# Seven VectorE instructions in place of seven transfers for the column shifts of a deformable convolution's offsets

## What is computed

```python
def deform_conv(x, dw, pw, pwb, w, b):
    f = lax.conv_general_dilated(x, dw, (1, 1), 'SAME', feature_group_count=C, ...)   # 7 x 7, by channel
    off = lax.conv_general_dilated(f, pw, (1, 1), 'SAME', ...)                        # 1 x 1, C -> 18
    off = (off + pwb[None, :, None, None]) * OFFSET_SCALE
    py = yy + ky + off[:, :, 0]          # for each of the 9 taps of each pixel: where to sample
    px = xx + kx + off[:, :, 1]
    sampled = bilinear_gather(x, py, px) # four corners, weighted
    return einsum('bckhw,ock->bohw', sampled, w) + b

h = jax.nn.relu(group_norm(x, gn1_g, gn1_b))
h = deform_conv(h, dw1, pw1, pwb1, w1, b1)
h = jax.nn.relu(group_norm(h, gn2_g, gn2_b))
h = deform_conv(h, dw2, pw2, pwb2, w2, b2)
return h + x
```

## Time and profile before

| | before |
|---|---|
| median of three executions | 5673.94 us |
| the profiled execution: time, span | 5669.95 us, 5668.2 us |
| PE busy, share of the span | 5075.3 us, 90% |
| DVE busy | 4010.8 us, 71% |
| ACT busy | 2315.8 us, 41% |
| POOL busy | 3194.0 us, 56% |
| issues of L489, the shifts | 224 of 36.0 KB |

### The profile page before, as it was taken

How to read it: one execution, slowest core, us unless ns; L and a number is a source line. 1 busy time by engine, 2 the same in 40 slices (tenths; PEclk the granted TensorE clock), 3 DMA queues, 4 the chain that set the end, 5 groups by cost and what they waited for, 6 DMA issues and landing times. The chain is left out here.

```text
span 5668.2 us, 75917 instructions
## 1 busy us (share of the span) xinstructions
PE 5075.3 (90%) x23148; PEld 2371.7 (42%) x23148; DVE 4010.8 (71%) x6610; ACT 2315.8 (41%) x4208; POOL 3194.0 (56%) x2820
## 2 busy tenths in 40 slices
PE   7999999999899999999978868859996996999688
PEld 3333333333433333333347656635543553554344
DVE  4888888884588888888333332237866785787798
ACT  2444444443244444444211111125544553555455
POOL 0666666664066666666447757626645563664675
PEclk9999999999999999999978879879998997999899
DMA  2000000001000000000134435549978997998998
GB/s 71 1 1 1 1 1 1 1 1 49 13 1 1 1 1 1 1 1 1 43 91 127 123 112 163 150 167 390 377 297 313 381 388 276 388 390 335 363 410 358
DMA packets 354547, 820.52 MB, mean 145 GB/s; under 512 B 104366, under 2 KB 171828, under 8 KB 354030
## 3 DMA queue, kind: packets, MB, share of 16 engines
q0 software_dynamic: 193536, 679.59, 31.8%
q1 hardware_dynamic: 160750, 137.65, 7.5%
HBM read 708.40 MB, written 100.43 MB: 143 GB/s over the span
## 5 line engine op out<-in xcount | busy, mean ns | idle before, releaser
L662 POOL TENSOR_TENSOR arena<-arena 128x512 f32<-128x512 f32 x960 | 1406.9, 1465 | 828.3 <-ACT arena L1296 763.8
L1296 ACT ACTIVATE arena<-ps 128x1024 f32<-128x1024 f32 x1024 | 1049.6, 1025 | 1239.4 <-PE ps L843 1209.9
L1827 DVE TENSOR_REDUCE arena<-ps 128x2 f32<-128x1024 f32 x1024 | 1243.0, 1214 | 347.5 <-PE ps L817 347.4
L714 POOL DMA_INDIRECT arena<-corners,arena x1152 | 1092.6, 948 | 685.2 <-issue 299.1
L2059 DVE SCALAR_TENSOR_TENSOR ps<-arena,ps 128x256 f32<-128x256 f32 x2304 | 955.8, 482 | 350.2 <-DVEq L2053 339.7
L1171 PE MATMUL ps<-arena 128*128 128x512 f32 x2304 | 1046.8, 598 | 0.2
L843 PE MATMUL ps<-arena 64*128 64x512 f32 x4096 | 1046.0, 589 | 0.0
L856 PE MATMUL ps<-arena 128*64 128x512 f32 x4096 | 991.4, 605 | 0.0
L1849 DVE TENSOR_TENSOR arena<-arena 128x512 f32<-128x512 f32 x960 | 888.5, 926 | 62.5 <-ACT arena L1296 62.1
L698 POOL DMA_INDIRECT arena<-corners,arena x576 | 545.9, 948 | 299.4 <-issue 245.7
L1483 ACT ACTIVATE ps<-arena 128x256 f32<-128x256 f32 x1152 | 497.2, 470 | 403.7 <-DMA arena<-corners,arena 193.5
(11 more groups left out here) (161 smaller groups left out, 3706.4 us busy)
## 6 DMA issues: line engine op xcount, KB each, us to landing
corners<-arena SPq DMA_DIRECT2D x256, 256.0 KB
arena<-corners,arena POOLq DMA_INDIRECT x1728, 8.9
img<-in_x SPq DMA_DIRECT2D x8, 1024.0 KB, 9.3
corners<-arena SPq DMA_DIRECT2D x128, 64.0 KB, 2.2
arena<-arena SPq DMA_DIRECT2D x224, 36.0 KB
arena<-in_wd SPq DMA_DIRECT2D x2, 2304.0 KB, 8.7
between<-img SPq DMA_DIRECT2D x4, 1024.0 KB, 5.9
arena<-between SPq DMA_DIRECT2D x4, 1024.0 KB, 9.5
```

Source lines behind the costliest of these rows:

```text
L662: pool.tensor_tensor(SUMS[u % 2][:, 0, :], SUMS[u % 2][:, 0, :], P[n % 4][:, 0, :], ALU.add).then_inc(sum_a, 1)
L714: pool.indirect_dma_start(G3[4 * k + t].rearrange("p a c -> p (a c)"), None, table256[b], bass.IndirectOffsetOnAxis(ap=IS3[:, k, t:t + 1], ...
L1296: af(P[n % 4].rearrange("p h q -> p (h q)"), ps[:, 2 * (n % 2):2 * (n % 2) + 2, :].rearrange("p h q -> p (h q)"), ACT.Exp, scale=float(D) ...
L1827: v.tensor_reduce(mxp[i % 2][:, :, j], ps[:, 4:6, :], AX.X, ALU.max).then_inc(mx_done, 1)
```

## The change

The 256-channel offsets use `side_shifts` as the 64-channel ones do: DVE reads PSUM bank 4 and writes T3, first the middle column tap with a 0/1 column as factor, then the six others, each added in place with its shift, each waiting for the one before. ACT's copy, SP's seven transfers, TP3 and its clearing on POOL are gone. On DVE the shifts stand after tap 1 of the next 256-channel block, or after the residual of tile 0 of the next 64-channel block; for the last block of a 256-channel stage after tap 8, of stage D at tile 2 of the block itself. PE's four small products move from tap 6 to tap 4 and wait for `t_ready` (now from DVE) and `side_bank` alone. DVE's `side_offsets3` moves from after tap 8 to after tap 7, and from tile 3 to tile 2.

```diff
@@ sync: tables_and_residuals, and the same in the three 256-channel stages
                     table_writes(0, n + 1, stage, table, cc)
-                    if cc == C:
-                        column_shifts()
                     keep_residual(b, n)
...
-            def column_shifts():
-                sp.wait_ge(rows_copied, 1)
-                sp.sem_inc(rows_copied, -1)
-                for kx in range(7):
-                    at = slice(kx * O3, (kx + 1) * O3)
-                    sp.dma_start(T3[at, :].rearrange("q (y x) -> q y x", x=W),
-                                 TP3[at, :].rearrange("q (y x) -> q y x", x=WP)[:, :, kx:kx + W]).then_inc(shifted_in, 16)
@@ tensor: products64 (side_shifted waits for side_bank alone), then products256
                         if q == at and not first:
                             side_shifts_done()
-                            side_shifted3()
+                            side_shifted(T3[0], 7, O3, sel3_s)
...
-                    if k == 6 and not first:
-                        side_shifted3()
+                    if k == 4 and not first:
+                        side_shifted(T3[0], 7, O3, sel3_s)
@@ scalar: copies64, then copies256
-                        if q == 0 and not first:
-                            side_rows_copy()
-                        if q == 2 and last:
-                            side_rows_copy()
...
-                    if k == 1 and not first:
-                        side_rows_copy()
...
                 output(NCH - 1)
-                if side is not None:
-                    side_rows_copy()
@@ vector
+            def side_shifts3():
+                side_shifts(7, T3[0], sel3_s, O3)
@@ vector: sums64
-                    if q == 0 and side == 64:
-                        side_shifts2()
-                    if q == (2 if side == 64 else 3):
+                    if q == 0:
+                        (side_shifts2 if side == 64 else side_shifts3)()
+                    if q == 2:
                         (side_offsets2 if side == 64 else side_offsets3)(n - 1)
...
-                        if last and q == 2 and side == 64:
-                            side_shifts2()
+                        if last and q == 2:
+                            (side_shifts2 if side == 64 else side_shifts3)()
@@ vector: sums256
-                        if side is not None and not first and k == 8:
-                            side_offsets3(g - 1)
+                        if side is not None and not first:
+                            if k == 1:
+                                side_shifts3()
+                            if k == 7:
+                                side_offsets3(g - 1)
...
                 if side is not None:
+                    side_shifts3()
                     side_offsets3(NCH - 1)
```

More of the change, by code:

```diff
@@ L154, in program @@
         BASE3 = off.f32(NT, O3)
-        WP = W + 6
-        T3 = off.f32(CHUNK, parts=7 * O3)
-        TP3 = off.f32(8 * WP, parts=7 * O3)
+        T3 = [off.f32(CHUNK, parts=7 * O3)]
         OFF3 = off.f32(NT, O3)
@@ L528, in _ @@
             go()
-            table_writes(0, 0, TS3, table256[0], C)
-            with sp.Fori(0, NCH - 1) as n:
-                table_writes(0, n + 1, TS3, table256[0], C)
-                column_shifts()
-            column_shifts()
+            with sp.Fori(0, NCH) as n:
+                table_writes(0, n, TS3, table256[0], C)
             sp.wait_ge(ts_free[0], 16 * 8)
@@ L543, in _ @@
             go()
-            table_writes(0, 0, TS3, table256[1], C)
-            with sp.Fori(0, NCH - 1) as n:
-                table_writes(0, n + 1, TS3, table256[1], C)
-                column_shifts()
-            column_shifts()
+            with sp.Fori(0, NCH) as n:
+                table_writes(0, n, TS3, table256[1], C)
             sp.wait_ge(ts_free[0], 16 * 8)
@@ L997, in side_shifted @@
                 last.then_inc(off_ready, 1)
-            def side_shifted3():
-                pe.wait_ge(shifted_in, 16 * 7)
-                pe.sem_inc(shifted_in, -16 * 7)
-                pe.wait_ge(side_bank, 1)
-                pe.sem_inc(side_bank, -1)
-                for t in range(4):
-                    last = mm(ps[:, 5, t * O3:(t + 1) * O3], T3[:, t * 128:(t + 1) * 128],
-                              sel3_s[:, 7:7 + O3], start=True, stop=True)
-                last.then_inc(off_ready, 1)
             def side_shifts_done():
@@ L1393, in side_copy3 @@
                 side_copy(TS3[:, 2 * part:2 * part + 2, :], 2 * C, part == 0, part == 1)
-            def side_rows_copy():
-                act.wait_ge(t_ps, 1)
-                act.sem_inc(t_ps, -1)
-                af(TP3.rearrange("q (y x) -> q y x", x=WP)[:, :, 3:3 + W],
-                   ps[0:7 * O3, 4, :].rearrange("q (y x) -> q y x", x=W), ACT.Copy).then_inc(side_copied, 1)
-                act.wait_ge(side_copied, 1)
-                act.sem_inc(side_copied, -1)
-                act.sem_inc(t_ready, 1)
-                act.sem_inc(rows_copied, 1)
             def copies64(side):
@@ L1422, in activated, with beside @@
                     af(H2[p], ps[0:CB, 2, 0:128], ACT.Relu, scale=bnf[:, 2:3], bias=bnf[:, 3:4]).then_inc(h2_ready, 1)
-                def beside(n, q, first, ahead, last):
+                def beside(n, q, ahead, last):
                     if side == 64:
@@ L1439, in beside, with four @@
                             side_normal(1, n + 2, q - 2)
-                def four(n, first=False, ahead=True, last=False):
+                def four(n, ahead=True, last=False):
                     for q in range(4):
@@ L1446, in four @@
                         activated(q % 2)
-                        beside(n, q, first, ahead, last)
+                        beside(n, q, ahead, last)
                 af(IS2.rearrange("p a k -> p (a k)"), IDX2[:, 0:4, :].rearrange("p a k -> p (a k)"), ACT.Copy).then_inc(is_ready, 4)
@@ L1461, in copies64 @@
                 staged2(0, 0)
-                four(0, first=True)
+                four(0)
                 with act.Fori(1, NCH - 2) as n:
@@ L1511, in output, with beside @@
                                bias=vec_s[:, B2, oh:oh + 1]).then_inc(evicted, 1)
-                def beside(n, k, first, ahead, last):
-                    if k == 1 and not first:
-                        side_rows_copy()
+                def beside(n, k, ahead, last):
                     if 2 <= k <= 3 and not last:
@@ L1530, in nine @@
                         if side is not None:
-                            beside(g, k, first, ahead, last)
+                            beside(g, k, ahead, last)
                 weights(0, 0)
```

9 lines of the change are left out of this document (removed).

## The result

The changed kernel takes 5589.23 us (median of four executions, 5586.15 to 5590.97), the kernel before 5673.19 us in the same series: a ratio of 0.9853, 95% interval 0.9836 to 0.987. The profiled execution has a span of 5584.4 us against 5668.2.

| | before, us | after, us | gain | forecast |
|---|---|---|---|---|
| stage D, first table transposes to the end of its statistics | 447.6 | 401.5 | 46 | 21 |
| stages E to G, from there to the statistics after G | 1502.5 | 1467.4 | 35 | 31 |

A forecast was written before the change was run, and what follows sets the result against it. PE was taken to bound stages E to G. Blocks 0, ends 30.9 and stage D 21 made 52 us off 5669.95: 5618, forecast as 5622 because that execution lay 4 us below the median; range 5596 to 5650.

The forecast's parts named there:

- The price of the shifts: Each shift on DVE takes 0.74 us, seven take 5.2 us; bounds 3.6 and 6.7 us.
- Blocks of E to G: Blocks of E to G: 3.5 us gained in E and F, 3.5 lost in G, nothing in sum.
- DMA relief: Stage G blocks: without the shifts' transfers DVE's gaps should hold; loss 3.5 us taken, bounds 0 and 7.1.
- The sign for E to G: The prediction fails if stages E to G are each not 9 to 11 us shorter.
- The ends of E to G: Ends of E, F and G: DVE's addition comes 10.3 us earlier each, 30.9 us in all, bounds 28 and 31.
- Stage D (a): Tile 0: bank 5 freed a tile earlier, PE's wait before table transposes 2.1 us shorter in five blocks, 10 us.
- (b): Stage D, tile 1: PE's 0.81 us wait for ACT's table copy behind the row copy goes, 4 us.
- (d): Stage D, last block and very end: shifts finish sooner, 1.8 and 1.4 us, together 3 us.
- (c), the clock: Stage D: excess of PE's 32 transposes after the tile 0 gap at lower clock; 4 us taken, bounds 0 and 8.6.
- More of stage D's clock comes back: Rival: 18 us beyond (c), the clock, giving 5604 us; 12% together with the DMA rival.
- DMA is the bound: Rival: each of 21 blocks gives back 1.6 us, 34 us more, 5588 us; 12% together with the clock rival.
- DVE did not make the kernel slower: Rival, E to G blocks: DVE late at tap 2, 5660 us, or 5731 without any gap; 15%, of it 6% slower.

The follow-up runs named there:

- e13: The changed kernel itself, unmodified, run and profiled again: 5589.31 us.
- e6: Changed kernel plus seven transfers of the old size and place in 7 blocks each of stages E, F and G, awaited by no compute engine: 5590.80 us.
- e7: Changed kernel with the last block's shifts in stages E, F and G waiting until ACT has copied out the last output block: 5610.25 us.
- e4: Changed kernel with stage D's addition of the offsets back behind the statistics of tile 3, shifts still on DVE: 5604.32 us.
- e5: Changed kernel with one spare ACT copy at tile 0 of each stage D block, bringing back a short PE stop at tile 1: 5612.26 us.
- e16: Changed kernel with the spare ACT copy of e5, and both halves of the next normalised block made at tile 2, removing tile 0's stop: 5602.07 us.
- e15: Changed kernel with five shift instructions instead of seven in the blocks of E, F and G (two column taps left out): 5570.17 us.
- e14: Changed kernel; stage D shifts ahead of the same block's tile 3 residual (tile 2 in the last), both normalised halves at tile 2: 5575.33 us.
- e17: Changed kernel with the seven shifts in blocks of E, F and G split: five after tap 1, two after tap 2: 5587.05 us.

## Why the prediction was wrong, step by step

- **The price of the shifts** was right: 0.735 and 0.743 us against 0.74, seven in 5.36 us.
- **Blocks of E to G**, put at nothing in sum. At tap 2 it is 0.28 us, as worked out for E and F (0.27), and DVE is no later than before in stage G. From block to block it is 54.73 us in all three stages, before mostly 55.0 in E and F and 54.9 in G: some 4 us. Two blocks of 56.7 before are gone as well, 3.4 us, but that is luck: the changed kernel has one of 56.4 when it is profiled again (e13). The first part of a stage took some of it back and differs by 2 us between two profiles of the changed kernel (134.5 and 132.6 us between the last small products of E and the first of F). What is left of all this is 3.5 us (35.1 less 31.7 at the ends). I had overlooked the 0.85 us that PE waited before its table transposes behind the row copy; it moved into the wait at tap 2, which is 1.69 us where the sign was 1.0 to 1.3. The reason given for G, DMA relief, is not borne out: e6's transfers don't bring a loss. What made DVE late there in the earlier trace rows stays open.
- **The sign for E to G**, each 9 to 11 us shorter, was met by one of three. Between the ends of the statistics they are 11.8, 10.3 and 13.0 us shorter: the ends as forecast, the rest from the items above.
- **The ends of E to G** were right: 10.56 us each, 31.7 for 30.9, and in e7 21 us of it are lost again.
- **Stage D (a)**: right in size. The five stops went from 12.5 to 3.7 us, 8.9 for 10; the next late was ACT's block, but 0.72 behind and not 0.3 to 0.6.
- **(b)**: 4.8 us for 4.
- **(d)**: 1.6 us at the small products, 1.8 at the end, 3.4 for 3.
- **(c), the clock, is the step that failed.** The sum took 4 us, with bounds of 0 and 8.6 for tile 0, "and some 14 more if tiles 1 and 2 stay at the high clock too". Those 14 are the excess of five blocks at tile 1 (5.7 us) and in the products of tile 2 (8.0 us); it was in the trace, but stood at nothing in the sum and only as a rival, with no reason given why it should stay. What came back is nearly all of it: the excess of the table was 27.2 us before and is 1.6 in the profile after (one group of 5.37 us; 4.6 in e13), so 25.6 us, and 1.4 more in the products of the last block. Two things were wrong. The cause was put on the stop that showed most, 2.45 us at tile 0, where by e4 a stop of 2.34 us costs 0.95 us in the transposes and 0.45 in the small group ahead of them, and nothing later. And the stop at tile 1 was priced at its own length, 0.81 us: by e5 and e16 a stop of 0.57 us there goes with two to three us of excess a block (14.1 and 18.8 us in six blocks). The range also left out the first of the six blocks, whose excess before was 5.0 us though its stop at tile 0 was 0.72 us alone. With 23 us more in (c) the sum is 75 of 84 us, with the 3.5 us of the blocks and 1 of the ends 79. The rest, some 4 us, was not added up one by one; in it are the 2 us ahead of stage D and PE's small groups that took longer, as the table transposes with 1.09 and not 0.63 us in two of six blocks at tile 1.
- **The rivals.** "More of stage D's clock comes back" is what happened, with 23 us beyond (c) and not 18; together with DMA's rival it had 12%. "DMA is the bound" gave 5588, the time measured, and is false by e6: a right number is no evidence for its mechanism. The time lies at 5588 through items that have nothing to do with DMA, which is luck. DVE did not make the kernel slower, but PE waits for it at tap 2: by e15 two instructions fewer give 0.85 us a block.

## What to carry to other kernels

Before a wait is priced by its length, compare the durations of PE's same group in every place of a block, not only right behind the wait: here much of what went with a short stop at tile 1 stood in the products of tile 2, some 10 us later. Add all of that excess to the range of any change that removes or makes a stop, and profile the same kernel twice before a slow block is put down to the change. And when work is moved to another engine, look for the place where that engine waits anyway ahead of what is late (e14), and check the first and the last block of the loop, whose order differs (e17).

## What the runs showed of the hardware

- A stop of 0.57 us of PE at tile 1 went with 1.2 to 1.6 us more in the next 32 transposes and 1.5 to 1.7 us more in 14 products some 10 us later: in all six blocks of e5, in four and five of six of e16. A stop of 2.34 us at tile 0 went with 0.45 us more in the table transposes and 0.95 in the 32 transposes right behind, and nothing later (e4). Why the place matters so much stays open: no run moved the same stop alone from tile to tile, and none took away the 0.88 us that PE waits in every tile.
- With no stop over 0.34 us at these places the products still took 7.95 and 7.77 us in two of six blocks, and 7.95 in the last one (e14), so these stops are not the only cause.
- DVE's shifts with a PSUM source take 735 ns each on 126 partitions (488 to 504 elements), as on 81 partitions (738 ns for 504); the first, with 512 elements, takes 743.
- 147 transfers of 36 KB in pieces of 256 B beside the gathers cost nothing that can be measured (e6), at a DMA share of 0.93 to 0.97.
